# A graph-layer stack on one core: degrees and first aggregation put into one stage that works by blocks

## The reference, cut to what matters

```
h       = relu(layernorm(x))
support = h @ W0.T + b0                                  # 4096 x 128
deg     = (adj + I).sum(axis=1)                          # 4096
x       = x + dinv[:, None] * ((adj + I) @ (dinv[:, None] * support)),  dinv = deg ** -0.5
h       = relu(layernorm(x));  z = h @ W1.T + b1         # input of the second layer,
                                                         # whose columns are normalised over all 4096 rows
```

## Time and profile before

| | |
|---|---|
| median of 3 runs | 2116.53 us (2115.51 to 2118.55) |
| the profiled execution, its time | 2119.51 us |
| the profiled execution, its span | 2117.7 us |
| PE, DVE, ACT busy, share of the span | 89%, 79%, 69% |
| mean granted clock of TensorE | 0.983 of full speed |

### The profile page before, as it was taken

How to read it: one execution, slowest core, us unless ns; L and a number is a source line. 1 busy time by engine, 2 the same in 40 slices (tenths; PEclk the granted TensorE clock), 3 DMA queues, 4 the chain that set the end, 5 groups by cost and what they waited for, 6 DMA issues and landing times.

```text
span 2117.7 us, 22055 instructions
## 1 busy us (share of the span) xinstructions
PE 1883.4 (89%) x7997; PEld 1199.4 (57%) x7997; DVE 1680.8 (79%) x2502; ACT 1466.5 (69%) x1541; POOL 0.8 (0%) x7
## 2 busy tenths in 40 slices
PE   2335999799988989889999989899999999999997
PEld 1224888578878888865555556544444444444443
DVE  4668989698878889887878853598889888988985
ACT  3445666456668989887878630498878788887873
POOL 0000000000000000000000000000000000000000
PEclk9999999899999999999999999999999999999999
DMA  9999898578875766658989778533232333323320
GB/s 388 429 428 369 334 343 337 195 282 317 318 296 199 253 241 231 241 213 329 333 329 354 300 294 300 172 114 122 94 127 102 112 104 110 119 101 127 103 76 11
DMA packets 81563, 489.51 MB, mean 231 GB/s; under 512 B 8449, under 2 KB 12546, under 8 KB 36402
## 3 DMA queue, kind: packets, MB, share of 16 engines
q1 hardware_dynamic: 77138, 485.94, 62.2%
q10 hardware_dynamic: 4320, 2.20, 0.4%
HBM read 452.36 MB, written 35.75 MB: 230 GB/s over the span
## 4 chain that ended last, share of the span: by engine, by line
PE 42%; DVE 8%; ACT 1%; issue 1%; DMA 0%; DVEq 0%; ACTq 0%
PE bank L1729 25%; PE bank L1691 5%; DVE work L1375 3%; PE bank L1605 2%; DVE reg L1375 1%; PE bank L1610 1%; PE bank L1611 1%; PE bank L1612 1%; PE bank L1634 1%; PE bank L1635 1%; DVE work L1353 1%; PE bank L1711 1%; PE bank L1598 1%; PE bank L1637 1%; PE bank L1636 1%
## 5 line engine op out<-in xcount | busy, mean ns | idle before, releaser
L1729 PE MATMUL bank<-work,reg 128*128 128x512 f32 x960 | 421.9, 595 | 17.3 <-DVE ring L1324 11.4
L1375 DVE TENSOR_TENSOR work<-work,ring 128x1536 f32<-128x1536 f32 x160 | 280.2, 1751 | 68.2 <-ACT work L784 67.4
L1729 PEld LDWEIGHTS bank<-work,reg 128*128 128x128 f32 x960 | 181.7, 191 | 245.8 <-issue 219.0
L962 DVE TENSOR_TENSOR a_lo<-ring,a_hi 128x2048 fp32r<-128x2048 f32 x128 | 290.8, 2287 | 31.4 <-ACT a_hi L553 30.5
L553 ACT ACTIVATE a_hi<-ring 128x2048 fp32r<-128x2048 f32 x128 | 244.3, 1913 | 76.1 <-PE bank L1533 76.1
L1565 PE MATMUL bank<-reg,ring 128*128 128x129 f32 x2048 | 244.8, 281 | 36.9 <-DVE ring L1076 36.8
L1565 PEld LDWEIGHTS bank<-reg,ring 128*128 128x128 f32 x2048 | 238.6, 197 | 42.4 <-DVE ring L1076 32.5
L784 ACT ACTIVATE work<-work 128x1536 f32<-128x1536 f32 x160 | 235.3, 1471 | 26.1 <-DVE work L1353 26.1
L1729 PE MATMUL bank<-reg 128*128 128x512 f32 x576 | 252.7, 592 | 0.0
L1531 PE MATMUL bank<-a_hi,s_hi 128*128 128x512 f32 x512 | 207.4, 405 | 20.1 <-DVE a_lo L962 20.1
L1533 PE MATMUL bank<-a_hi,s_lo 128*128 128x512 f32 x512 | 201.9, 394 | 0.0
(11 more groups left out here) (232 smaller groups left out, 2680.7 us busy)
## 6 DMA issues: line engine op xcount, KB each, us to landing
ring<-in_adj_units SPq DMA_DIRECT2D x320, 1024.0 KB, 4.9
ring<-in_adj_rows SPq DMA_DIRECT2D x32, 2048.0 KB, 17.0
ring<-masks SPq DMA_DIRECT2D x64, 512.0 KB, 4.6
masks<-work SPq DMA_DIRECT2D x48, 512.0 KB, 9.0
masks<-ring SPq DMA_DIRECT2D x16, 512.0 KB, 8.2
reg<-lines SPq DMA_DIRECT2D x8, 768.0 KB, 10.0
ring<-lines SPq DMA_DIRECT2D x8, 768.0 KB, 8.0
out<-ring ACTq DMA_DIRECT2D x8, 256.0 KB, 2.3
```

Source lines behind the costliest of these rows:

```text
L962: dve.tensor_tensor(a_lo[:, ring_at(p, g)], ring[:, ring_at(p, g)], a_hi[:, (g % 4) * UNIT:(g % 4 + 1) * UNIT].bitcast(F32), ALU.subtract) ...
L1375: dve.tensor_tensor(tv, tv, spread(ring[:, ring_at("out", g, q * W, W)], HEADS, 1), ALU.mult).then_inc(s_y, 1)
L1729: last = pe.matmul(bank[1 + k][:, :], h, tiles(c * T + t)[:, k * W:(k + 1) * W], start=t == 0, stop=t == T - 1)
```

## The change

There are no longer two stages. The neighbours are taken in eight blocks g of 512. For a block, its four row tiles are loaded as eight halves of 1 MiB and summed, its four degrees (and `dinv`) are made, its 512 rows of `support` are scaled into `reg1`, and then its eight units, one for each chunk c, are multiplied. The sums of all eight chunks stay open in the eight PSUM banks over the whole stage. The list `STREAM` sets the order of all loads: the row halves of block g+2 come behind the units of block g, except that only four units of block 0 stand ahead of the rows of block 1, and that the rows of block 7 are in two halves, behind the units of block 5 and of block 6. Each load n waits until load n-8, in the same slot, has been used.

The products are plain float32: a 128x128 piece of the unit is the weights, the scaled support (128 columns) is what moves, 16 matmuls to a unit, so that the sum has nodes in the partitions and needs no turning. `a_hi`, `a_lo`, `s_hi`, `s_lo` are no longer made in this layer. The eight row halves of block 0 are summed by ACT alone, two for each of the first four chunks of support; from block 1 on DVE sums one half of a tile and ACT the other, but both only behind their work for all eight chunks of support. The layer norm, turn and projection behind the aggregation (`layer_turn`, `layer_project`) stand among the units of block 7. The cell weights (`gru`) are loaded later, and small constants are made on DVE behind the third chunk's norm.

```
@@
-def over_chunks(eng, body):
-    body(0, True)
-    with eng.Fori(1, C) as c:
-        body(c, False)
+STREAM = block_rows(0) + block_units(0)[:Q] + block_rows(1) + block_units(0)[Q:] + block_rows(2)
+for block in range(1, G - 3):
+    STREAM += block_units(block) + block_rows(block + 2)
+STREAM += block_units(G - 3) + block_rows(G - 1, 0, Q) + block_units(G - 2) + block_rows(G - 1, Q) + block_units(G - 1)
@@ SP
-            for s in range(4):
-                sp.dma_start(ring[:, s * N:(s + 1) * N], rows_d[s * P:(s + 1) * P, :]).then_inc(s_rows[s], 16)
-            with sp.Fori(1, C) as c:
...
+            for n, (kind, g, i) in enumerate(STREAM):
+                if n >= G:
+                    given_back(n % G, STREAM[n - G])
+                if kind == "row":
+                    load_row(g, i)
+                else:
+                    load_unit(g, i)
+                if n == 2 * G:
+                    sp.dma_start(gru[:, :], gru_d).then_inc(s_gru, 16)
@@ ACT
+            root("deg", 0)
+            for c in range(C):
+                if c == Q:
+                    degree_root(0)
+                if c + 1 < C:
+                    root("deg", c + 1)
+                if c < Q:
+                    row_sum(c, 0)
+                    row_sum(c, 1)
+                support_hT(c)
+                support_keep(c)
+            for g in range(1, G):
+                for q in range(Q):
+                    row_sum(g * Q + q)
+                degree_root(g)
@@ DVE
+            for c in range(C):
+                norm_in(s, c)
+                if c:
+                    dve.wait_ge(s_hturn["deg"], c)
+                s.inc(norm_out(s, "deg", c, c + 1))
...
+                if c == 2:
+                    constants()
+                if c == Q:
+                    degrees(0)
+            for g in range(1, G):
+                for q in range(Q):
+                    row_sum(g * Q + q)
+                degrees(g)
@@ PE
+            def block(g, c):
+                pe.wait_ge(s_scale["agg0"], g + 1)
+                slot, count = block_slot(g, c)
+                pe.wait_ge(s_unit[slot], count)
+                for q in range(Q):
+                    for i in range(Q):
+                        o, t = bank[c][:, i * P:(i + 1) * P], g * Q + q
+                        first = slot * UNIT + q * W + i * P
+                        last = pe.matmul(o, ring[:, first:first + P],
+                                         reg1[:, t * P:(t + 1) * P], start=t == 0 and i == 0,
+                                         stop=t == T - 1 and i == Q - 1)
+                    if q == 0 and g == c:
+                        for i in range(Q):
+                            t = c * Q + i
+                            pe.matmul(bank[c][:, i * P:(i + 1) * P], ident[:, :], reg1[:, t * P:(t + 1) * P],
+                                      start=False, stop=False)
+                last.then_inc(s_mm["agg0"], 1)
...
+            for c in range(Q + 1):
+                support(c)
+            for g in range(G):
+                for c in range(C):
...
+                    block(g, c)
+                    if g == 0 and Q + 1 + c < C:
+                        support(Q + 1 + c)
+                    if g == G - 1 and c > 2:
+                        layer_project(c - 3)
+                    if g == G - 1 and c > 1:
+                        layer_turn(c - 2)
```

More of the change, by code:

```diff
@@ L41 @@
 MASKS = 4
+ROWS_AHEAD = 2
 MLOADS = 8
@@ L377, in load @@
+            user = {block_slot(G - 1, c)[0]: ("agg0", block_unit(G - 1, c)) for c in range(C)}
             def load(p, n):
                 slot = n % SLOTS[p]
[L380 to L384, removed]
+                sp.wait_ge(*unit_read(*user[slot]))
                 user[slot] = (p, n)
@@ L405, in load_masks @@
                 sp.dma_start(kept[b][2], masks_d[n * P:(n + 1) * P, :]).then_inc(s_mload[b], 16)
-            for p in ("agg0", "agg1", "gat"):
+            for p in ("agg1", "gat"):
                 for n in range(C * G):
@@ L470, in root @@
                 act.activation(rstd[:, Q:2 * Q], rstd[:, 0:Q], ACT.Sqrt).then_inc(s_root[p], 1)
[L472 to L493, removed]
             def project_keep(p, c):
@@ L1436, in project @@
                 pe.wait_ge(s_hT[p], c)
-                if p == "deg":
-                    if not (isinstance(c, int) and c == 1):
-                        pe.wait_ge(s_pkeep[p], c - 1)
-                    for q in range(Q):
-                        o = bank[4][:, q * P:(q + 1) * P]
-                        pe.matmul(o, ones[0:1, :], rows[0:1, 0:P], start=True, stop=False)
-                        last = pe.matmul(o, hT[:, q * P:(q + 1) * P], w0t, start=False, stop=True)
-                elif p == "agg0":
-                    pe.wait_ge(s_pkeep["deg"], C)
-                    pe.wait_ge(s_pkeep[p], c - 1)
-                    last = pe.matmul(bank[4][:, :], w1t, hT[:, :], start=True, stop=True)
-                elif p == "agg1":
+                if p == "agg1":
                     pe.wait_ge(s_pkeep["agg0"], C)
@@ L1466, in project, with support @@
                 last.then_inc(s_proj[p], 1)
-            def deg_body(c, first):
-                turn_h("deg", c + 1)
-                project("deg", c + 1)
-            pe.wait_ge(s_ln["deg"], LN_STEPS["deg"])
-            turn(bank[3], hn).then_inc(s_hturn["deg"], 1)
-            project("deg", 1)
-            with pe.Fori(2, C + 1) as c:
-                turn_h("deg", c)
-                project("deg", c)
+            def support(c):
+                pe.wait_ge(s_ln["deg"], (c + 1) * LN_STEPS["deg"])
+                if c:
+                    pe.wait_ge(s_hT["deg"], c)
+                turn(bank[6], hn).then_inc(s_hturn["deg"], 1)
+                pe.wait_ge(s_hT["deg"], c + 1)
+                if c:
+                    pe.wait_ge(s_pkeep["deg"], c)
+                for q in range(Q):
+                    o = bank[7][:, q * P:(q + 1) * P]
+                    pe.matmul(o, ones[0:1, :], rows[0:1, 0:P], start=True, stop=False)
+                    last = pe.matmul(o, hT[:, q * P:(q + 1) * P], w0t, start=False, stop=True)
+                last.then_inc(s_proj["deg"], 1)
@@ L1497, in own_rows @@
                     pe.matmul(o, s_lo[:, t * P:(t + 1) * P], ident_r[:, :], start=False, stop=False)
-            for p in ("agg0", "agg1"):
+            for p in ("agg1",):
                 def turn_bn(g):
```

320 lines of the change are left out of this document (197 added, 123 removed).

## The result

The changed kernel takes 2134.68 us (median of 5 runs, 2128.43 to 2136.24) against 2116.53 us: ratio 1.0081, 95% interval 1.0069 to 1.0094, 18.2 us more. On another chip it was 2137.68 against 2117.24, ratio 1.0091 (1.0075 to 1.0107). The forecast was slower by 8.3 us, 2125 us. The sign was right. The size was less than half of what was measured, and 2134.68 lies 0.7 us above the forecast's own range of 2118 to 2134 (inside the wider one, 2104 to 2146).

The account below looks back on a forecast made before the run. Transfers bound the old kernel up to 173 us, then PE to 386; the new stage's waits along the path summed to `bn_aggr` at 407.0, 8.3 us later, so 2125 us, own range 2118 to 2134, wider 2104 to 2146.

Parts of the forecast that it names:

- Blocks 1 to 4: Blocks 1 to 4 of the merged stage: 39.3 us each on PE, 39.2 for transfers, together 157.3 us, to 299.4.
- a term put at nothing: Code behind `bn_aggr`: same code and same length as before, so only the start of `bn_aggr` counts.
- The opening, to 73.4: Start to the end of the fifth support projection: first projection at 21.3, periods of 11.75 us, end at 73.4.
- First four units, 31.9: Block 0's first four units with the last three chunks of support: 31.9 us, ending at 105.3.
- Fifth unit's wait, 7.4: PE before block 0's fifth unit: 7.4 us of waiting for a load one behind a row half.
- Block 1 at 142.1: Start of block 1: its first unit comes 12 loads, 29.4 us, after the fifth unit's landing at 112.6.
- Blocks 5 to 7, 97.6: Last three blocks: PE no longer waits; units 91.0 us plus turns and projections 6.6, to 397.0.
- Behind the last unit, 10.0: From the last unit to `bn_aggr`: add, norm, turn, relu, projection and statistics take 10.0 us, to 407.0.
- The sum, 8.3: `bn_aggr` at 407.0 against 398.7 before, 8.3 us later.
- The opening at full clock: Rival for the opening: projections take 3.4 us, the five save 12.3, giving 2112.5 us; chance 0.24.
- A slower PE: Rival for the units: 3.86 us each, 17 us more on the path, 2142 us; chance 0.13.
- Slower transfers: Rival for loads in the mix: 2.93 us each, a block 46.9 us, 2165 us in all; chance 0.05.

Follow-up runs that it names:

- relu_first: Changed kernel with ACT's relu ahead of its two row sums in the first four chunks; 2119.36 us, ratio to before 1.0001.
- the second profile: The changed kernel timed and profiled again with no edit; 2137.68 us, ratio to before 1.0091, `bn_aggr` at 414.6.
- packed_rows: Changed kernel with the adjacency by rows laid out so that each 1 MiB row half is one contiguous piece; 2134.87 us, ratio to before 1.0075.
- no_bias: Changed kernel without the one-row matmuls that add b0 to support, in all eight chunks; 2104.41 us, ratio to before 0.9942.
- bias_dve: Changed kernel with ACT's relu ahead of its row sums and b0 added by DVE instead of one-row matmuls; 2098.10 us, ratio to before 0.9905.
- the thin blocks: Changed kernel with a quarter of the products left out in blocks 1 to 6; 2132.44 us, ratio to before 1.0060.

## Why the sign was right, and which steps of the sum failed

That the changed kernel is slower came for the reason given: the opening's chain holds up the ring, and `relu_first`, which shortens that chain and nothing else, takes the same 14.6 us from both the first product and `bn_aggr`.

**Two steps of the sum failed.** The first is the transfers' term in *Blocks 1 to 4*: 16 x 2.45 = 39.2 us a block at the 428 GB/s of the large row tiles, taken as level with PE's 39.3, so 157.3 us for four. The runs show 160.9 us at 417 GB/s and 165.6 us at 408. The second is a term put at nothing: that all behind `bn_aggr` stays of the same length, so that the stage's difference could be added to the median of before. Of the 18.2 us between the medians, 12.0 lie in the stage by the first profile, 2.7 are a longer stretch behind it in the profiled execution, 3.0 are what the profiled execution of before lay above its median, and 0.4 what the median of the changed kernel lay above its profiled execution. The miss of nearly 10 us is thus 3.7 in the stage and 6.1 outside it; by the second profile, with `bn_aggr` 15.9 us later, it is 7.6 in the stage.

The terms one by one, measured in the first profile unless said otherwise:

- *The opening, to 73.4*: 69.7. The chain was as said; a period took 11.1 instead of 11.75, since neighbouring instructions on ACT overlap by 0.1 us, which I had added as hand-overs. That the relu edit shortens the whole by just what it takes from the opening shows the mechanism.
- *First four units, 31.9*: 33.5 (69.7 to 103.2). A projection at full clock took 3.4, as I chose. But the clock fell again: the granted clock reads 0.50 from 80 to 82 us, and the second and third unit took 4.96 and 5.37 us instead of 3.6. My sum had that loss once, at the first unit:

```profile
80.55 4.96 PE L1585 MATMUL bank<-reg,ring 128*128 128x128 f32 x32
...
89.87 5.37 PE L1585 MATMUL bank<-reg,ring 128*128 128x128 f32 x32
```

- *Fifth unit's wait, 7.4*: 7.8. *Block 1 at 142.1*: 142.2, which is luck. The opening was set 3.7 us too long, and the units behind it, the wait and the 12 loads (31.1 instead of 29.4 us) together 3.8 too short.
- *Blocks 1 to 4, 157.3*: **the term of the stage that was mis-sized.** 160.9 in the first profile, 165.6 in the second; 160.8 to 164.1 in the other variants that keep this part (packed_rows, relu_first, no_bias, bias_dve). I had PE's 39.3 and the transfers' 39.2 us as level, and took 428 GB/s for both layouts. With 8 KB pieces a load takes not 2.45 but 2.49 us (422 GB/s), 0.6 us more to a block; the step from there to 2.51 and 2.57 us (417 and 408), up to 1.4 us a block, is not explained. So a block takes 40 to 41.4 us. Transfers hold it there even with a quarter of PE's work gone, but PE's own side was close: a block's products took 31.2 to 32.5 us, and with the 7.8 us that a unit takes to come back that makes 39.0 to 40.3. The loads of blocks 5 to 7 run at much the same rate (415 GB/s from 290 to 360 us).
- *Blocks 5 to 7, 97.6*: 98.1 (303.1 to 401.2). The number held, its reason only half, and that is luck in part: PE has no wait for a transfer there, as I said, but leaving out PE's work brought nothing, since the degrees of block 7 come no earlier.
- *Behind the last unit, 10.0*: 9.6 (401.1 to 410.7).
- *The sum, 8.3*: `bn_aggr` came 12.0 and 15.9 us later in the two profiles. The part outside the stage is not shown to come from the change: before has its stage at 398.7 in both profiles, with 1719.0 and 1722.4 us behind it, and the stretch behind varies from 1715 to 1724 us over all kernels. Which part of the 18.2 us lies in the stage of a median execution no run shows, since no median execution was profiled. As an estimate, 2134.7 less 1.8 and less the mean stretch of 1719 puts `bn_aggr` near 414, as in the second profile; the same sum for before gives 396 where 398.7 was measured twice, so it is good to some 3 us.
- *Rivals.* The opening at full clock falls: 0.79 and 0.80 us for the pairs from first to last, in `relu_first` too. The rule of "TensorE: Matmul & The Clock Gate", Part 1, in the Trainium skill, that sustained activity releases the throttle, does not show on these projections, but does on the units behind them: from 69.67 on, 8 records take 1.91 us at first, and a projection at 76.95 starts at full clock. A slower PE falls too, with 3.6 us a unit; the thin blocks test only a faster one, and with the 0 to 1.6 us a block that PE's waits had above 7.8 us, a slower one would have cost time. Slower transfers: right in kind, 408 to 422 GB/s instead of 358. That figure of "DMA: Bandwidth & Descriptors", Specifications, in the Trainium skill, is not what this core was held to: the lowest rate from 115 to 290 us with a share of 1.00 was 408.

What stays open: why the rate differs between executions of the same kernel (408 and 417 GB/s over the same 175 us), why it lies below the 422 GB/s of 8 KB pieces alone (the mix of the two streams, or PE's work, of which the 421 GB/s of the thin blocks are a hint), whether it is the size of the pieces or the number of transfers that takes 1.4%, and how the 18.2 us divide in a median execution.

## What to carry to other kernels

When stages are merged so that transfers may run through, ask which load is the first to wait for an engine: a ring in program order stands still with it, and here each microsecond of that engine's opening was a microsecond of the whole, with transfers at 152 GB/s from 70 to 110 us. Look there for work that shares an in-order list with the chain without belonging to it (two row sums ahead of a relu: 14.6 us), and for small work inside the chain (a one-row matmul for a bias: 27 us over eight chunks by the first profile). And where two bounds come out level to a tenth of a microsecond, price the rate of the one with the piece size that the new code uses. Profile more than one execution of before, too, ahead of adding a difference of a few us to its median: the stretch behind the change, in unchanged code, took 1715 to 1724 us here.

## What was not expected of the hardware

- A matmul of one row between full ones costs more than its own work. Four pairs (one-row bias, then 128x128) took 5.8 us at the low clock and 3.4 at the high one; the four full ones by themselves 2.08 and 1.16. At the low clock the timeline of PE's weight loads shows a gap of 0.22 to 0.23 us between those of one matmul and the next in the pairs, and none in the projection without bias. Why is not shown. In the kernel before, then in the projection of `no_bias` at 27.82:

```profile
32.31 0.49 PEld L1442 LDWEIGHTS bank<-reg,ones 1*128 1x128 f32 x2 [7.29 <-ACT hT L478]
33.03 0.50 PEld L1443 LDWEIGHTS bank<-wts,hT 128*128 128x128 f32 x2 [0.23 <-issue]
33.75 0.50 PEld L1442 LDWEIGHTS bank<-reg,ones 1*128 1x128 f32 x2 [0.23 <-issue]
...
27.82 1.78 PEld L1572 LDWEIGHTS bank<-wts,hT 128*128 128x128 f32 x8 [4.80 <-ACT hT L555]
```

- The transfer rate of the same program varied between executions by more than 2% (408 to 417 GB/s) where 8 KB pieces were moved with the queue full, while the 16 KB pieces of before gave 428 in both profiles.
